# Routed expert block: other routing instructions, the first fetch issued ahead of other work, and rows gathered as fp32 and split into fp16 halves tile by tile

## The reference, cut to what matters

```python
x = x + tanh(g_xattn) * xattn(layernorm(x), ctx, desc_router, W_q, b_q, itok)   # top 2 of 64 sets
xf = layernorm(x).reshape(-1, 256)
logits = xf @ gate_w + gate_b
top_val, top_idx = top_k(logits, 2)                 # 2 of 8 experts
gate_score = softmax(top_val)
comb[e, t] = sum_k gate_score[t, k] * (top_idx[t, k] == e) * alpha[e]
for e in range(8):                                  # hidden size 1024
    out += comb[e][:, None] * (gelu(xf @ fc1_w[e] + fc1_b[e]) @ fc2_w[e] + fc2_b[e])
x = x + tanh(g_ffn) * out
```

## Time and profile before

| | us |
|---|---|
| median of 3 runs (335.35 to 339.35) | 335.55 |
| the profiled execution's own time | 335.43 |
| its span, first to last instruction | 333.7 |
| mean granted TensorE clock, share of full | 0.864 |

### The profile page before, as it was taken

One profiled execution on the slowest core, in us unless ns is written; L12 is line 12 of the kernel. 1 busy time (PEld: TensorE's weight loads), 2 busy tenths in 40 slices (PEclk: granted clock), 3 DMA queues, 4 the chain that ended last, 5 costly groups with the idle time before them and its releaser, 6 DMA issues.

```text
span 333.7 us, 9399 instructions
## 1 busy us (share of the span) xinstructions
PE 263.3 (79%) x3110; PEld 245.1 (73%) x3110; DVE 211.7 (63%) x648; ACT 168.8 (51%) x466; POOL 158.9 (48%) x126
## 2 busy tenths in 40 slices
PE   3999934223107999999999999999999999999920
PEld 3988833112106999989999999999999999989920
DVE  5988689889576787576557755676564454544400
ACT  2062474353332867556765676567654444444500
POOL 5211108877060075556555655664664646462430
PEclk9995555555556999999999999999999999999995
DMA  5999999913032125454434546343535544446211
GB/s 167 349 372 380 373 380 373 321 47 130 0 73 57 35 42 86 72 78 68 80 67 81 78 84 78 59 79 68 87 65 93 67 80 69 79 59 74 33 17 15
DMA packets 47696, 40.17 MB, mean 120 GB/s; under 512 B 24113, under 2 KB 44354, under 8 KB 47650
## 3 DMA queue, kind: packets, MB, share of 16 engines
q1 hardware_dynamic: 39520, 28.85, 29.8%
q0 software_dynamic: 7488, 10.39, 20.0%
q10 hardware_dynamic: 642, 0.33, 0.4%
HBM read 25.07 MB, written 9.37 MB: 103 GB/s over the span
## 4 chain that ended last, share of the span: by engine, by line
PE 59%; DVE 17%; DMA 7%; ACT 6%; issue 5%; DVEq 1%; ACTq 1%; POOL 0%; POOLq 0%
PE bank L577 25%; PE bank L595 22%; DMA out_dram<-xn,add_at 5%; DVE wreg L1177 4%; PE bank L427 4%; ACT rows L805 2%; ACT wreg L740 2%; PE bank L413 2%; DVE rows L968 1%; DMA xs<-in_x_dram 1%; ACT xn L717 1%; DMA xTp<-xs 1%; PE bank L455 1%; PE bank L589 1%; DVEq L1173 1%
## 5 line engine op out<-in xcount | busy, mean ns | idle before, releaser
L577 PE MATMUL bank<-xTp,wreg 128*128 128x128 f16 x1872 | 154.4, 221 | 3.7 <-issue 2.4
L595 PE MATMUL bank<-wreg,rows 128*128 x936 | 150.7, 273 | 0.0
L577 PEld LDWEIGHTS bank<-xTp,wreg 128*128 x1872 | 130.2, 99 | 12.8 <-issue 5.7
L805 ACT ACTIVATE rows<-bank,maskbias 128x128 f32<-128x128 f32 x312 | 88.8, 368 | 87.5 <-PE bank L577 47.2
L1327 POOL DMA_INDIRECT out_dram<-xn,add_at x39 | 77.7, 1992 | 90.0 <-ACT xn L815 62.1
L595 PEld LDWEIGHTS bank<-wreg,rows 128*128 128x128 f16 x936 | 80.6, 98 | 4.6 <-DVE rows L1250 0.3
L1248 DVE TENSOR_SCALAR rows<-rows 128x512 f16<-128x512 f32 x78 | 33.3, 427 | 59.5 <-ACT rows L805 59.5
L1319 POOL DMA_INDIRECT xs<-xrows,fetch_at x39 | 44.4, 1138 | 31.4 <-DVE fetch_at L1114 11.3
L1250 DVE SCALAR_TENSOR_TENSOR rows<-rows 128x512 f16<-128x512 f32 x78 | 54.0, 693 | 2.7
L1177 DVE SCALAR_TENSOR_TENSOR wreg<-wreg x16 | 36.7, 2292 | 18.2 <-ACT wreg L740 13.3
L740 ACT ACTIVATE wreg<-wreg x16 | 30.6, 1911 | 15.9 <-issue 10.2
(11 more groups left out here) (196 smaller groups left out, 203.5 us busy)
## 6 DMA issues: line engine op xcount, KB each, us to landing
wreg<-in_L_ffn_fc_w_dram SPq DMA_DIRECT2D x16, 1024.0 KB, 13.4
xrows<-rows SPq DMA_DIRECT2D x4, 528.0 KB, 4.1
xs<-in_x_dram SPq DMA_DIRECT2D x4, 512.0 KB, 9.3
out_dram<-xs SPq DMA_DIRECT2D x4, 512.0 KB, 7.9
xs<-xrows,fetch_at POOLq DMA_INDIRECT x39, 3.8
xTp<-xs SPq DMA_TRANSPOSE x39
out_dram<-xn,add_at POOLq DMA_INDIRECT x39, 4.3
ctx_sb<-in_ctx_dram SPq DMA_DIRECT2D x1, 512.0 KB, 9.4
```

The lines of the kernel that those rows point to most:

```text
L577: mm = pe.matmul(put, w, xT[:, i % NX, x_part, k, :], start=(k == 0 and n == 0), stop=(k == KC - 1 and n == 2))
L595: mm = pe.matmul(yb, h, w, start=False, stop=(c == FC - 1 and n == 2))
L805: op = act.activation(h32[i % 2][:, f * P:(f + 1) * P], bank[2 * (i % 2) + half][:, c * P:(c + 1) * P], ACT.Gelu, bias=b1cur[:, i % NX, f: ...
```

## The change

Four edits. (1) Routing: `max_index`, the cast, the one-hots and the pair weights go; `match_replace` marks the two chosen experts, four ACT exponentials per group (`gexp`) give the softmax, `slots` takes the places by `max`, and `weigh_sets` no longer sums the set weights: a column of ones in `ctxgw` makes PE do it, and the reciprocal moves to the head of `add_attention`, behind a wait for both gate matmuls. (2) `normalise` writes fp32 rows to `rows`; the fp16 copy L728 and the four `row_low(g)` go. (3) Opening: ACT copies `tokens_at` ahead of the first weight conversion; the matmul for all 39 tiles moves behind tile 0 on PE and its read-out into `table_adds`, behind tile 0's splits on DVE; `unit_regions` loads one value, not two. (4) Main loop: ACT's new `row_high(i)` makes the fp16 high half of a gathered tile, DVE's new `row_low(i)` the low half, both into `xh`, and SP transposes from there. In the loop they are called for tile i + 3 (AHEAD = 3), on ACT behind `gelu(i, 1)`, on DVE behind `split(i, 1)`. POOL's order is as it was; only what a fetch waits for differs.

```diff
+    AHEAD = 3
+    G2 = E + 2
...
-        ctxgw = sb("ctxgw", [P, NG, G1])
+        ctxgw = sb("ctxgw", [P, NG, G2])
...
-        xg_h = xg.bitcast(F16)
+        xh = xs[:, 2 * NXG:4 * NXG, :].rearrange("p t d -> p (t d)")[:, 0:NXG * D].bitcast(F16).rearrange("p (s a d) -> p s a d", s=NXG, a=2)
...
             def keep_rows(g):
-                sp.wait_ge(row_ready, g + 1)
+                sp.wait_ge(xn_done, (g + 1) * GT)
+                sp.wait_ge(comb_ready, g + 1)
                 sp.dma_start(xrows_t[:, g * GT:(g + 1) * GT, :], rows[:, g, :, :]).then_inc(rows_out, 16)
...
-                sp.wait_ge(xg_in[i % NXG], (i // NXG + 1) * 16)
+                sp.wait_ge(row_lo, i + 1)
                 sp.dma_start_transpose(xT[:, i % NX, :, :, :].rearrange("p a k q -> p (a k) q"),
-                                       xg_h[:, i % NXG, 0:2 * D]).then_inc(xT_in[i % NX], 16)
+                                       xh[:, i % NXG, :, :].rearrange("p a d -> p (a d)")).then_inc(xT_in[i % NX], 16)
...
             pe.matmul(bank[6][:, 0:PER_RANK], tokens_at[:, :], is_col[:, 0:PER_RANK], start=True, stop=True).then_inc(fetch_ps, 1)
-            pe.wait_ge(cols_ready, 2)
-            pe.matmul(bank[6][:, 0:TILES], tokens_at[:, :], is_col[:, :], start=True, stop=True).then_inc(fetch_ps, 1)
...
                 tile(i, ws[i + 2], ws[i + 1], ws[i])
+                if i == 0:
+                    pe.wait_ge(cols_ready, 2)
+                    pe.matmul(bank[6][:, 0:TILES], tokens_at[:, :], is_col[:, :], start=True, stop=True).then_inc(fetch_ps, 1)
...
             def squares(g):
-                if g >= 2:
-                    act.wait_ge(row_ready, g - 1)
...
             def normalise(g):
...
-                    act.activation(xn[:, g % 2, t, :], xs[:, n, :], ACT.Identity, bias=shift2[:, n:n + 1],
+                    act.activation(rows[:, g, t, 0:D].bitcast(F32), xs[:, n, :], ACT.Identity, bias=shift2[:, n:n + 1],
                                    scale=rs16[:, n:n + 1]).then_inc(xn_done, 1)
-                act.wait_ge(xn_done, (g + 1) * GT)
-                act.activation(rows[:, g, :, 0:P].bitcast(F16), xn[:, g % 2, :, :], ACT.Copy).then_inc(hi_ready, 1)
 
             def route_exp(g):
-                act.wait_ge(gdiff_ready, g + 1)
-                act.activation(gediff[:, g % 2, :], gdiff[:, g % 2, :], ACT.Exp).then_inc(gexp_ready, 1)
+                act.wait_ge(gneg_ready, g + 1)
+                for t in range(GT):
+                    op = act.activation(gexp[:, t, :], logit[:, t, :], ACT.Exp, bias=gneg[:, t:t + 1])
+                op.then_inc(gexp_ready, 1)
+
+            region_now = [NU]
             def unit_regions(k):
-                return [act.value_load(units_i[0:1, j:j + 1], min_val=0, max_val=NU) for j in (k + 1, k)]
+                put = region_now[0]
+                region_now[0] = act.value_load(units_i[0:1, k + 1:k + 2], min_val=0, max_val=NU)
+                return region_now[0], put
...
+            act.wait_ge(tokens_ps, NG)
+            act.activation(tokens_at[:, :], bank[1][:, 0:P], ACT.Copy).then_inc(tokens_sb, 1)
             act.wait_ge(units_ready, 2)
             for u in range(NU):
                 act.wait_ge(w_in[u], 16)
             weights_hi(0, unit_regions(0))
-            act.wait_ge(tokens_ps, NG)
-            act.activation(tokens_at[:, :], bank[1][:, 0:P], ACT.Copy).then_inc(tokens_sb, 1)
             at = unit_regions(1)
             act.activation(tg_gelu[:, :], gcol[:, :], ACT.Gelu)
-            weights_hi(1, at)
+
+            def row_high(i):
+                if i >= NXG:
+                    act.wait_ge(xT_in[i % NX], (i // NX) * 16)
+                act.wait_ge(xg_in[i % NXG], (i // NXG + 1) * 16)
+                act.activation(xh[:, i % NXG, 0, :], xg[:, i % NXG, 0:D].bitcast(F32), ACT.Copy).then_inc(row_hi, 1)
...
+            row_high(0)
+            weights_hi(1, at)
+            for i in range(1, AHEAD):
+                row_high(i)
             for i in range(TILES):
                 if i == TILES - 1:
                     weigh(i - 2)
                 gelu(i, 0)
                 if 2 <= i < TILES - 1:
                     weigh(i - 2)
                 gelu(i, 1)
+                if i + AHEAD < TILES:
+                    row_high(i + AHEAD)
                 for k in units_of_tile.get(i, ()):
                     weights_hi(k, unit_regions(k))
...
             def weigh_sets(g):
...
-                v.tensor_reduce(den[:, :], wset[:, :, :], AX.X, ALU.add).then_inc(vec_step, 1)
-                v.reciprocal(den[:, :], den[:, :]).then_inc(vec_step, 1)
...
             def add_attention(g):
+                gates = bank[4][:, 2 * P:2 * P + GT * G2].rearrange("p (t e) -> p t e", t=GT)
...
+                v.wait_ge(gate_ps, 2 * g + 2)
+                v.reciprocal(den[:, :], gates[:, :, G1]).then_inc(vec_step, 1)
+                v.wait_ge(vec_step, done.up())
+                v.tensor_scalar(scale_a[:, g, :], den[:, :], tg[:, 0:1], None, ALU.mult).then_inc(vec_step, 1)
...
-            def row_low(g):
-                v.wait_ge(hi_ready, g + 1)
-                v.tensor_tensor(rows[:, g, :, P:2 * P].bitcast(F16), xn[:, g % 2, :, :], rows[:, g, :, 0:P].bitcast(F16),
-                                ALU.subtract).then_inc(row_ready, 1)
...
+                v.tensor_scalar(gneg[:, :], gtop[:, :, 0], -1.0, None, ALU.mult).then_inc(gneg_ready, 1)
+                v.tensor_copy(gtwo[:, :, 0:2], gtop[:, :, 0:2]).then_inc(vec_step, 1)
+                v.wait_ge(vec_step, done.up())
                 for t in range(GT):
-                    v.max_index(gtopi[:, t, :], gtop[:, t, :], logit[:, t, :]).then_inc(vec_step, 1)
+                    v.match_replace(gmark[:, t, :], gtwo[:, t, :], logit[:, t, :], CHOSEN).then_inc(vec_step, 1)
                 v.wait_ge(vec_step, done.up(GT))
-                v.tensor_copy(gtop2f[:, :, :], gtopi[:, :, 0:2]).then_inc(vec_step, 1)
+                v.tensor_single_scalar(picks[:, r, :], gmark[:, :, :], CHOSEN, op=ALU.is_equal).then_inc(vec_step, 1)
...
+                v.tensor_tensor(comb[:, :, :], picks[:, r, :], gexp[:, :, :], ALU.mult).then_inc(vec_step, 1)
...
+                v.tensor_reduce(gden[:, :], comb[:, :, :], AX.X, ALU.add).then_inc(vec_step, 1)
...
             def slots(g):
...
+                for t in range(GT):
+                    v.max(slot_f[:, t, :], pick_slots[:, t, :]).then_inc(vec_step, 1)
...
             def table_adds():
+                v.wait_ge(fetch_ps, 2)
+                v.tensor_copy(fetch_at[:, PER_RANK:TILES], bank[6][:, PER_RANK:TILES]).then_inc(fetch_ready, 1)
...
+            def row_low(i):
+                v.wait_ge(row_hi, i + 1)
+                v.tensor_tensor(xh[:, i % NXG, 1, :], xg[:, i % NXG, 0:D].bitcast(F32), xh[:, i % NXG, 0, :],
+                                ALU.subtract).then_inc(row_lo, 1)
...
+            def between():
+                weights_lo(0, first_unit)
+                row_low(0)
+
+            table_tiles(between)
             fetch(0)
+            row_low(1)
             weights_lo(1, unit_regions(1))
-            table_adds()
+            row_low(2)
             for i in range(TILES):
                 if i + 1 < TILES:
                     fetch(i + 1)
                 split(i, 0)
                 split(i, 1)
+                if i + AHEAD < TILES:
+                    row_low(i + AHEAD)
+                if i == 0:
+                    table_adds()
...
             def fetch_rows(i):
                 if i >= NXG:
-                    pool.wait_ge(xT_in[(i - NXG) % NX], ((i - NXG) // NX + 1) * 16)
+                    pool.wait_ge(row_lo, i - NXG + 1)
                     pool.wait_ge(cur_ready, i - NXG + 1)
```

More of the change, by code:

```diff
@@ L159, in flamingo_block @@
         gtop = sb("gtop", [P, GT, 8])
-        gtopi = sb("gtopi", [P, GT, 8], U32)
-        gtop2f = sb("gtop2f", [P, GT, 2])
-        gdiff = sb("gdiff", [P, 2, GT])
-        gediff = sb("gediff", [P, 2, GT])
+        gtwo = sb("gtwo", [P, GT, 8])
+        gneg = sb("gneg", [P, GT])
+        gmark = sb("gmark", [P, GT, E])
+        gexp = sb("gexp", [P, GT, E])
         gden = sb("gden", [P, GT])
-        gpair = sb("gpair", [P, GT, 2])
-        onehot = sb("onehot", [P, GT, 2, E])
-        oh_tmp = sb("oh_tmp", [P, GT, 2, E])
         comb = sb("comb", [P, GT, E])
+        pick_slots = sb("pick_slots", [P, GT, E])
         picks = sb("picks", [P, NT, E])
         earlier = sb("earlier", [P, NT + 1, E])
-        slot_f = sb("slot_f", [P, GT, 2])
+        slot_f = sb("slot_f", [P, GT, 8])
         slot_i = sb("slot_i", [P, GT * 2], I32)
@@ L301, in flamingo_block @@
         xn_done = sem("xn_done")
-        hi_ready = sem("hi_ready")
-        row_ready = sem("row_ready")
-        gdiff_ready = sem("gdiff_ready")
+        comb_ready = sem("comb_ready")
+        row_hi = sem("row_hi")
+        row_lo = sem("row_lo")
+        gneg_ready = sem("gneg_ready")
         gexp_ready = sem("gexp_ready")
@@ L435, in attention @@
```

(40 more changed lines are left out.)

58 lines of the change are left out of this document (19 added, 39 removed).

## The result

The changed kernel takes 440.49 us (median of 4 runs, 439.91 to 441.89) against 335.45 for the kernel before, run on the same chip (334.65 to 339.35). The ratio is 1.3155, with a 95% interval from 1.3119 to 1.3191: slower by a little less than a third. The forecast was 455 us, and the measured time lies inside its range of 424 to 500. The profiled execution took 441.89 us, its span is 440.1, so 1.8 us lie around it. Medians here are of all runs of a kernel, ratios of the undisturbed ones on both sides (single runs, far off at 383 to 568 us, are left out there), so a ratio can stand a little off that of two medians.

The account below looks back on a forecast made before the run. PE bounded the kernel before; the change was to make a closed ACT-POOL chain the bound. First fc1 94.1, y(0) 17.4 later, 34 periods of 8.4 (285.6), weights 25.2, end 31.2, plus 1.7 around: 455 us, range 424 to 500.

Parts of the forecast that it names:

- the circle: Main loop, ACT and POOL: y(i - 2), add, fetch, landing, row_high, y(i - 1) form a closed chain of 8.4 us; chance 0.80.
- add to fetch: On POOL, from the start of an add to the next fetch: 2.31 us, or 1.85 by the least add.
- `row_high` to y: On ACT, row copy 0.5 us, then gelu start to weigh start 1.02 us; 2.1 us more in weight tiles.
- the landing: Time from POOL's fetch until the gathered tile has landed: median 3.8 us, from 2.9 to 4.8.
- Weights on the circle: On ACT between row_high and the next gelu, a weight conversion adds 2.1 us in 12 tiles, 25.2 us in all.
- DVE's part: In the opening, removed row_low and sums less new waits and longer slots: 3.2 us earlier, bounds 1.5 and 5.5.
- The tail from y(34): End of the kernel, set by the adds as before: 31.2 us from y(34) to the end of the span.
- Half clock: Rival: PE's pauses in the loop drop it to 1.2 GHz, at most 10.8 us per tile, 537 us; chance 0.10.
- Landing hidden: Rival: rows are there when gelu(i, 1) ends, so ACT's row_high does not wait: 327 us; chance 0.06.
- gain given back: Rival: landing hidden, but new copies on DVE and ACT delay handovers by 8 us: 335 us, no change; chance 0.04.
- The rule and the row: Fetch landing by the skill's rule, 2.3 us (period 6.9, time near 404), against the measured rows, 2.9 to 4.8 us.
- POOL beside DVE: DVE's second split beside POOL's add could lengthen an add by up to 0.4 us, the time by some 15 us; not included.

Follow-up runs that it names:

- two edits that each open the circle: Two runs on the changed kernel: AHEAD 2 instead of 3, 344.31 us; POOL issuing each fetch one add earlier with AHEAD 3, 333.91 us.
- `old_routing`: `fetch_ahead_start_again` with the new routing taken back to that of the kernel before: 332.06 us, ratio 0.9822.
- `fetch_ahead_start_again`: Changed kernel with fetches one add earlier, table read-out ahead of the loop, fetch 4 not waiting for the add table, weight conversion before row copy; repeat run: 332.65 us.
- `fetch_ahead`: Changed kernel with AHEAD still 3, but POOL issues each fetch one add earlier (fetch i + 5 ahead of add i): 333.91 us, ratio 0.9916.

## Why the prediction was right, step by step

**The mechanism** was the one forecast, with its place (ACT's wait in `row_high`) and its other half (POOL behind y). It is shown by two edits that each open the circle, on ACT's side and on POOL's.

**The sum.** From the timelines of ACT and POOL, y(0) to y(34) took 295.9 us: 22 periods without a weight conversion of 8.14 us in the mean, 12 with one of 9.74. By the terms of the prediction (means of the 22 and of the 12):

| step | forecast | without weights | with weights |
|---|---|---|---|
| y to its add | 0.77 | 0.77 | 0.77 |
| add to fetch | 2.31 | 2.60 | 2.35 |
| fetch to `row_high` | 3.8 | 3.44 | 3.13 |
| `row_high` to y | 0.5 + 1.02, + 2.1 with weights | 1.32 | 3.50 |
| sum | 8.4, 10.5 | 8.14 | 9.74 |

The mis-sized term is the landing. I took the median of before, 3.8 us; in the kernel after it is:

```profile
DMA to landing us min/median/max: 2.7/3.0/4.9
```

Landing got shorter as the DMA share fell from 0.46 to 0.27 (the two windows above); that the one causes the other is my reading, no run tested it. The mean counts here, not the median: the gathers of the 22 periods landed after 3.36 us, those of the 12 after 3.04, and the copy began 0.08 us later. So the step is off by 0.36 and 0.67, not by 0.8. `row_high` holds ACT 0.32 us to the next start, not 0.5. Against these, add to fetch is longer, 2.60. Together the 34 periods took 14.9 us less than the 310.8 forecast (285.6 + 25.2).

**Weights on the circle.** 3.50 - 1.32 = 2.18 us each on ACT, as forecast (2.1). That the two kinds of period differ by only 1.6 us doesn't mean that a conversion costs 1.6. Of the 22 periods without one, 12 follow a weight tile, and their add begins while DVE's `weights_lo` of that tile is under way: add to fetch is 2.81 us there and 2.35 in the other ten. So a conversion costs 2.18 us in its own period and 0.46 in the next, for which the sum had nothing.

**Opening and ends.** First fc1 95.65 against 94.1: 1.55 late. The first fetch went out at 88.41 instead of 86.4, 2.0 late, and the steps from it to fc1 took 7.24 us instead of 7.7. The term at fault is DVE's part: 3.2 us forecast; `slots(3)` began at 79.06 instead of 80.50 and `is_col` at 86.68 instead of 87.94, 1.3 to 1.4 us, a little under my lower bound of 1.5. The 1.22 us of `row_low(3)` that went there came back as DVE's wait of 1.22 us for PE's ranks, in the fence above; the same wait in the groups before (0.63 us each in groups 1 and 2) took more of the gain than I had allowed. y(0) came 19.0 behind the first fc1, not 17.4: fetch 4 went out at 10.6 us (10 forecast), and its copy began 4.9 us behind it (106.23 to 111.15), not 3.8. The tail from y(34) took 29.5, not 31.2. The span then is 453.5 + 1.55 + 1.6 - 14.9 - 1.7 = 440.05, measured 440.1. That the time is only 3% off is in part luck: the terms missed in both directions.

**Routing.** I had taken the routing itself as even and the two sums over the set weights as a gain of 0.8 us. Alone, edit 1 gained nothing. `old_routing` is 0.6 us under `fetch_ahead_start_again` by the medians, and by the ratios (0.9822 against 0.9937) more; both pairs speak for a small loss by the new routing, of a size that they leave open. Which of its steps takes the gain back wasn't separated.

**The rivals.** *Half clock* was right that the clock falls, wrong in that it costs. Two windows of the circle at the two levels, 1.2 and 2.4 GHz:

```profile
325.97:329.81 3.84, 3.84 (x28) 3.28 (x27) 0.64 (x2) 0.70 (x3) 1.20 (x1) 0.50 0.43 69
330.64:334.40 3.76, 3.76 (x55) 3.57 (x52) 2.23 (x5) 1.31 (x5) 2.90 (x2) 1.00 0.46 49
```

The first stretch follows five microseconds (321 to 326) in which PE was busy for 1.1. PE does half the matmuls there. But `row_high` to y stayed at 1.32 us in all 22 periods and at 3.49 to 3.50 in the 12: PE's work was there in time, and the lower clock only filled its idle time. *Landing hidden* would have needed another order of POOL. With that order (`fetch_ahead`) the time is 333.9 us, which is *gain given back* (335) more than 327: hidden landings alone did not keep the gain of the opening.

**The rule and the row.** The shortest landing took 2.7 us. The estimate of 2.3 us from the Trainium skill, "DMA: Bandwidth & Descriptors", section "Anatomy of one DMA", was reached by no fetch. For POOL beside DVE the start decides. Three adds with the DVE instruction in which each began, the first pair from the kernel before (L1250 there is L1252 here, the second step of a split):

```profile
286.00 0.69 DVE L1250 SCALAR_TENSOR_TENSOR rows<-rows 128x512 f16<-128x512 f32 x1
...
134.32 0.69 DVE L1252 SCALAR_TENSOR_TENSOR rows<-rows 128x512 f16<-128x512 f32 x1
134.42 2.03 POOL L1339 DMA_INDIRECT out_dram<-xn,add_at  x1 [4.81 <-ACT xn L826]
...
142.52 2.29 DVE L1177 SCALAR_TENSOR_TENSOR wreg<-wreg  x1 [1.99 <-ACT wreg L746]
143.92 2.51 POOL L1339 DMA_INDIRECT out_dram<-xn,add_at  x1 [6.18 <-ACT xn L826]
```

The first is the add of 286.15. All three end a fixed time behind the end of that DVE instruction: 1.47, 1.44 and 1.62 us. It is so throughout the kernel after: 13 adds began inside a `weights_lo` and ended 1.62 us behind it, 20 began inside the second step of a split and ended 1.44 to 1.46 behind it, and the two that ran with DVE idle took 1.55. In the kernel before, adds that began inside a `weights_lo` took from 2.03 to 3.27 us, by how much of it was left, and ended 1.61 to 1.62 behind it. So the add seems to do its work only when the DVE instruction under way is over. By the Trainium skill, "SBUF — State Buffer", section "Who interferes with whom", one of the two has a shared port for its whole instruction and the other waits for it, and the rows agree, in size too. So the 15 us that I had put beside the sum were counted twice: the row of 286.15, 2.01 us, already held the wait for a split. What the sum lacked was `weights_lo`: add to fetch was 2.81 us in 13 periods and 2.35 in 20, some 7 us over the loop above my 2.31.

## What to carry to other kernels

When a wait is added to an engine that works in order, write down what that engine does behind the wait, and follow who waits for it: if the path comes back to the thing waited for, the loop has a least period which is the sum of the path, DMA latency included, and no engine's busy time tells of it. Then look one step ahead or back in each queue on the path: here three lines on POOL took back 105 us. A look-ahead has two ends: three tiles closed the circle, two left the transposing DMA 1 us too little.
